# A score tile of 128 keys made by four matmuls of 32 keys, in the column tiling of the weighted sums

## The chip, the cores and the metric

One NeuronCore of a Trainium2 chip. The metric is the device time of one execution in microseconds (us). A core has a matrix engine (TensorE, PE in the profile; its weight loads are PEld), VectorE (DVE), ScalarE (ACT), GpSimd (POOL) and SyncE (SP, which only starts transfers). TensorE writes into eight PSUM banks of 128 partitions x 512 f32.

## The reference

Eight batches. `x` is (8, 1024, 512), the context (8, 2048, 512), 16 heads of 32.

```python
xn = layer_norm(layernorm(x), g1, b1);  cn = layer_norm(context, g2, b2)
q, k, v = xn @ Wq.T, cn @ Wk.T, cn @ Wv.T            # 16 heads of 32
scores = einsum('bqhs,bkhs->bhqk', q, k) / sqrt(32)  # masked keys: -inf
attn = softmax(scores);  out = einsum('bhqk,bkhs->bqhs', attn, v)
x = x + out @ Wo.T + bo
x = x + fp6_quantised(layernorm(x)) @ fp6_quantised(weight).T + bias
```

## The kernel before, in words

Each engine has its program written out by hand; semaphores (`wait_ge`, `then_inc`) are all that orders them. A batch has three stages: projections of queries, keys and values (`front`), attention, and output tiles with the quantised layer.

Attention goes in 8 **units** a batch: a group of four heads (`g`) times half of the queries (`q`, 512). A unit takes the 2048 keys in 16 **tiles** of 128, one `step` each. For one tile and four heads j:

- **scores** (`score(j)`, L947): one f16 matmul of 98 rows (a head's 32 dimensions in three split parts, and two rows for the mask and the maximum) by 128 keys, streaming 512 queries, into one bank.
- **exponentials** (L743, ScalarE), one for each score bank, into `PR[u]`, a ring of four f32 tiles.
- **weighted sums** (`outputs()`, L957): four f32 matmuls, one a head, each with 128 rows by 32 columns, head j writing partitions 32j to 32j+31 of the bank `OB`. The four are column tiles of the array. An f32 matmul stands as two records in the profile, so that a step has eight.
- **maxima** (`max_pair`, L923): two pairs of f16 matmuls of 33 rows by 128 columns, which compute part of the scores of a later unit, from which VectorE takes row maxima (L583). All units but the last need them for the next: in a batch 104 of the 128 steps have them, the last half of unit 6 and all of unit 7 don't.
- **row sums** (L983): four matmuls like the weighted sums, with ones for weights. GpSimd adds exponentials of two tiles in pairs (`pair`, L399) and merges the pairs with accumulating transfers (`merge`, L410, `merge_late`, L416), so that row sums are needed in only four steps of a unit. In the last step of a unit there are two `clear` matmuls (L989) beside them.

A step issues scores 0 and 1 of the next tile, weighted sums of this tile, scores 2 and 3 of the next, maxima, row sums. Score j waits until its bank's last exponential is made: for tiles under 8 there are two score banks, so that score 1 waits for exponential 3 of the tile before; for the others three. The weighted sums wait for all four exponentials of their tile. The exponentials of an even tile wait until GpSimd has added the pair that last used their buffers. A maxima pair waits for the reduction before the last (two pairs of banks). GpSimd issues the second late merge of a unit when the first has landed, and only then takes the next unit's pairs.

Of the kernel before, what the change touches and what calls it, by code (L numbers as in the profile page):

```python
# [8 lines left out]
P = 128  # L9


def ds(start, n):
    return slice(start, start + n)


HALF = 512
# [32 lines left out]
def build(nc, x, ctx_in, mask, wqT, wkT, wvT, woT, bo, affine_in, w, wb, out):  # L49
    B, T, D = x.shape  # L50
    C = ctx_in.shape[1]
    H, HD = 16, D // 16
# [53 lines left out]
    with ExitStack() as es:  # L106
# [3 lines left out]
        KA = sb("keys_stacked", [P, H * C], F16)  # L110
        QA = sb("queries_stacked", [P, NU * J * HALF], F16)
# [53 lines left out]
        def score_bank(tile, j):  # L165
            if tile < 8:
                return bank(4 + j % 2), 2
            slot = 4 * (tile - 8) + j + ((tile, j) >= (10, 2))
            return bank((7, 4, 5)[slot % 3]), 2 if tile == 10 and j >= 2 else 3
# [37 lines left out]
        s_st = sem("scores_made")  # L207
# [622 lines left out]
        def _(e):  # L830
# [13 lines left out]
            for b in range(0, B):  # L844
# [72 lines left out]
                STR = 3 * HD + 2  # L917

                def max_pair(parity, g, q, r, h):
                    a, t, c = piece(r, h)  # L920
                    for i in range(2):
                        rows = ds(2 * HD * i, HD + 1)
                        mm = e.matmul(MXB[parity][:, i, :],  # L923
                                      QA[rows, ds(((2 * g + q) * J + 2 * a + i) * HALF + t * P, P)],
                                      KA[rows, ds((g * J + 2 * a + i) * C + c * HALF, HALF)], start=True, stop=True)
                    mm.then_inc(s_mxf, 1)
# [5 lines left out]
                def step(m, ex, ka, qa, v, u, tile, row=None, after=None, sums=(), end=False, between=None, scores=True,  # L932
                         weigh=True, fresh=None, closing=False, turning=True):
                    if row:
                        count, *piece_of = row
                    if after:
                        e.wait_ge(*after)

                    def score(j):
                        if scores:  # L940
                            dst, back = score_bank(tile, j)
                            e.wait_ge(s_ex, ex + (u + 1) * J + j + 3 - back)
                            if tile == 8 and j == 0:
                                e.wait_ge(s_on, m + 1)
                            if tile == 11 and j == 0 and turning:
                                e.wait_ge(s_mc, m + 2)
                            e.matmul(dst, KA[0:STR, ds(ka + (j * C + (u + 1) * P), P)],  # L947
                                     QA[0:STR, ds(qa[j], HALF)], start=True, stop=True).then_inc(s_st, 1)

                    def max_part(h):  # L950
                        e.wait_ge(s_mxd, count + (h + 1))
                        max_pair(h, *piece_of, h)

                    def outputs():
                        e.wait_ge(s_ex, ex + (u * J + J + 2))
                        for j in range(J):
                            mm = e.matmul(OB[HD * j:HD * j + HD, :], V[:, ds(v + u * D + HD * j, HD)],  # L957
                                          PR[u][:, j * HALF:j * HALF + HALF], start=False, stop=end,
                                          skip_group_check=True)
                        return mm  # L960

                    score(0)
                    score(1)
                    if weigh:
                        mm = outputs()
                        if end:
                            mm.then_inc(s_po, 1)
                    if between:
                        between()
                    score(2)  # L970
                    score(3)
                    if not weigh:
                        return
                    if row:
                        max_part(0)
                        max_part(1)
                    if fresh:
                        clear(LB, *fresh)
                    for i, (src, ready) in enumerate(sums):
                        if ready:  # L980
                            e.wait_ge(*ready)
                        for j in range(J):
                            mm = e.matmul(LB[HD * j:HD * j + HD, :], ones[:, :], src[:, ds(j * HALF, HALF)],  # L983
                                          start=False, stop=closing and i == len(sums) - 1, skip_group_check=True)
                    mm.then_inc(s_pv, 1)

                def clear(bank, left, count):
                    e.wait_ge(left, count)
                    e.matmul(bank[:, 0:2], zeros[:, :], zeros[:, 0:2], start=True, stop=False,  # L989
                             skip_group_check=True)  # L990
# [120 lines left out]
```

## Time and profile before

| | |
|---|---|
| median of 3 runs | 4893.51 us (4892.85 to 4898.69) |
| the profiled execution | 4894.66 us, its span 4892.9 us |
| TensorE busy | 4593.8 us, 94% |
| VectorE, GpSimd, ScalarE busy | 69%, 61%, 58% |
| score matmuls (L947) | 4096 |
| mean granted TensorE clock | 0.986 of 2.4 GHz |

The span is from the first to the last instruction. A record's duration is longer than the time it keeps the engine, because matmuls are pipelined: the start of one to the start of the next is what a matmul costs in a row of its kind.

### The profile page before, as it was taken

What the parts mean: (1) busy time and instruction counts of PE and PEld (TensorE: products, weight loads), DVE (VectorE), ACT (ScalarE), POOL (GpSimd) and SP (SyncE); (2) the same over time, 40 slices, a digit from 0 to 9 for tenths busy, and PEclk for the clock granted to TensorE, in tenths of its full rate; (3) what the DMA queues carried; (4) which work ended last, traced back from release to release, by engine and by line L of the source; (5) the groups of instructions that cost most, each with busy time, mean ns of one, the idle gap of its engine ahead of it and who ended that gap; (6) DMA issues with size and microseconds to landing.
All of it is one profiled execution on the core that took longest, in us unless ns stands there. A gap on an engine that the chain in (4) does not pass through costs nothing.

```text
span 4892.9 us, 65384 instructions
## 1 busy us (share of the span) xinstructions
PE 4593.8 (94%) x24720; PEld 1348.4 (28%) x24720; DVE 3379.8 (69%) x3943; ACT 2838.0 (58%) x5128; POOL 2971.8 (61%) x1818
## 2 busy tenths in 40 slices
PE   4999899998999989999899998999989999899998
PEld 2322242222422224222242222422224222342222
DVE  4788457884588855888357884588855887458873
ACT  3477634775347753477544774457744577446773
POOL 2278743777438773387634876347863578625875
PEclk9999999999999999999999999999999999999999
DMA  5255632555325553355533555335543355443552
GB/s 182 64 118 104 147 113 60 118 111 152 99 65 105 119 147 102 70 104 118 141 102 71 111 110 140 104 72 117 108 134 109 73 116 112 127 113 80 106 119 75
DMA packets 189918, 530.81 MB, mean 108 GB/s; under 512 B 28625, under 2 KB 102673, under 8 KB 148386
## 3 DMA queue, kind: packets, MB, share of 16 engines
q0 software_dynamic: 43776, 318.79, 32.3%
q1 hardware_dynamic: 145826, 207.83, 13.8%
q8 instruction: 195, 3.19, 0.3%
q14 instruction: 121, 0.99, 0.1%
HBM read 110.98 MB, written 21.01 MB: 27 GB/s over the span
## 4 chain that ended last, share of the span: by engine, by line
PE 75%; ACT 10%; DVE 6%; SPq 3%; DMA 3%; issue 2%; POOL 1%; ACTq 0%; DVEq 0%; POOLq 0%
PE banks L957 21%; PE banks L947 19%; PE banks L864 12%; PE banks L923 9%; PE banks L858 7%; ACT region L743 7%; PE banks L983 5%; DVE max_parts L583 3%; SPq L293 3%; PE banks L833 2%; DMA region<-in_x 1%; DVE region L574 1%; ACT values L814 1%; ACT region L718 0%; POOL wkT_wvT_wqT L399 0%
## 5 line engine op out<-in xcount | busy, mean ns | idle before, releaser
L583 DVE TENSOR_REDUCE max_parts<-banks 128x2 f32<-128x1024 f32 x2048 | 2400.1, 1218 | 469.2 <-PE banks L923 468.2
L743 ACT ACTIVATE region<-banks 128x512 f32<-128x512 f32 x4096 | 2211.0, 596 | 695.9 <-PE banks L947 656.9
L399 POOL TENSOR_TENSOR wkT_wvT_wqT<-region 128x1024 f32<-128x1024 f32 x608 | 1474.7, 2549 | 556.5 <-ACT region L743 554.3
L947 PE MATMUL banks<-queries_stacked,keys_stacked 98*128 98x512 f16 x4096 | 1298.4, 387 | 82.2 <-ACT region L743 50.7
L957 PE MATMUL banks<-region,values 128*32 128x512 f32 x8192 | 1100.6, 609 | 18.5 <-ACT region L743 7.7
L947 PEld LDWEIGHTS banks<-queries_stacked,keys_stacked 98*128 98x128 f16 x4096 | 289.0, 97 | 1438.7 <-ACT region L743 1356.4
L923 PE MATMUL banks<-keys_stacked,queries_stacked 33*128 33x512 f16 x4096 | 658.7, 384 | 7.0 <-DVE max_parts L583 3.5
L864 PE MATMUL banks<-region,wkT_wvT_wqT 128*128 128x512 f16 x2304 | 574.6, 388 | 48.1 <-POOL region L380 23.0
L601 DVE RECIPROCAL row_sums_inverse<-row_sums_inverse 128x128 f32<-128x128 f32 x256 | 232.0, 930 | 437.9 <-ACT row_sums_inverse L760 437.9
L399 POOL TENSOR_TENSOR sums<-region 128x1024 f32<-128x1024 f32 x160 | 395.7, 2631 | 25.7 <-ACT region L743 25.5
L574 DVE SCALAR_TENSOR_TENSOR region<-banks,region 128x512 f16<-128x512 f32 x192 | 132.2, 689 | 346.7 <-ACT region L726 345.7
L864 PE MATMUL banks<-wkT_wvT_wqT,region 128*128 128x512 f16 x1536 | 369.1, 380 | 0.0
L399 POOL TENSOR_TENSOR wdT<-region 128x1024 f32<-128x1024 f32 x128 | 314.4, 2595 | 1.5 <-ACT region L743 0.4
L923 PEld LDWEIGHTS banks<-keys_stacked,queries_stacked 33*128 33x128 f16 x4096 | 159.6, 93 | 559.9 <-issue 298.0
L726 ACT ACTIVATE region<-banks 128x512 f16<-128x512 f32 x192 | 113.7, 597 | 343.0 <-PE banks L864 286.2
L380 POOL TENSOR_TENSOR region<-row_sums_inverse,region 128x512 f16<-128x512 f32 x80 | 92.5, 1156 | 339.9 <-ACT region L718 339.9
L864 PEld LDWEIGHTS banks<-region,wkT_wvT_wqT 128*128 128x128 f16 x2304 | 214.6, 100 | 302.8 <-issue 65.0
L858 PE MATMUL banks<-wdT,values 128*128 128x512 f32 x512 | 249.8, 633 | 48.2 <-ACT values L814 48.2
L730 ACT ACTIVATE values<-banks 128x512 f32<-128x512 f32 x128 | 76.4, 597 | 334.0 <-PE banks L864 334.0
L858 PE MATMUL banks<-woT,queries_stacked 128*128 128x512 f32 x512 | 245.2, 627 | 26.3 <-DVE region L667 26.3
L416 POOL DMA_DIRECT2D wdT<-wkT_wvT_wqT x96 | 99.9, 1040 | 275.9 <-ACT region L743 155.3
L957 PEld LDWEIGHTS banks<-region,values 128*32 128x32 f32 x8192 | 161.6, 108 | 380.7 <-ACT region L743 219.3
(83 smaller groups left out, 2905.3 us busy)
## 6 DMA issues: line engine op xcount, KB each, us to landing
wdT<-wkT_wvT_wqT POOLq DMA_DIRECT2D x96, 1024.0 KB, 11.4
wkT_wvT_wqT<-wkT_wvT_wqT POOLq DMA_DIRECT2D x80, 1024.0 KB, 7.0
sums<-wkT_wvT_wqT POOLq DMA_DIRECT2D x72, 1024.0 KB, 7.0
keys_stacked<-region SPq DMA_DIRECT2D x768, 64.0 KB, 2.0
wkT_wvT_wqT<-sums POOLq DMA_DIRECT2D x40, 1024.0 KB, 7.0
region<-in_x SPq DMA_DIRECT2D x24, 1024.0 KB, 10.0
wkT_wvT_wqT<-weights_split SPq DMA_DIRECT2D x8, 3072.0 KB, 19.3
queries_stacked<-region SPq DMA_DIRECT2D x384, 64.0 KB, 2.0
```

Source lines behind the costliest of these rows:

```text
L293: e.dma_start(dst, KS[HD * j:HD * j + HD, part, gs, :]).then_inc(s_kd[h], 16)
L399: e.tensor_tensor(SUMS[dst][:, half], PR[i][:, half], PR[i + 1][:, half], ALU.add).then_inc(s_pr, 1)
L574: e.scalar_tensor_tensor(KS[:, 1, i, :], PJB[j % 2], 1.0 / W_SCALE, KS[:, 0, i, :], ALU.mult, ALU.subtract).then_inc(s_k2, 1)
L583: e.tensor_reduce(mpart[:, buf, :, a, t, c], MXB[parity], AX.X, ALU.max).then_inc(s_mxd, 1)
L601: inv = e.reciprocal(part, part)
L743: e.activation(PR[u % 4][:, j * HALF:j * HALF + HALF], score_bank(kt, j)[0], ACT.Exp, scale=SCALE).then_inc(s_ex, 1)
L858: mm = e.matmul(bank, lhs(cc), rhs(cc), start=(cc == 0), stop=(cc == CC - 1))
L864: mm = e.matmul(bank, lhs(p, cc), rhs(r, cc), start=(cc == 0 and i == 0), stop=(cc == CC - 1 and i == 2))
L923: mm = e.matmul(MXB[parity][:, i, :], QA[rows, ds(((2 * g + q) * J + 2 * a + i) * HALF + t * P, P)], KA[rows, ds((g * J + 2 * a + i) * C + ...
L947: e.matmul(dst, KA[0:STR, ds(ka + (j * C + (u + 1) * P), P)], QA[0:STR, ds(qa[j], HALF)], start=True, stop=True).then_inc(s_st, 1)
L957: mm = e.matmul(OB[HD * j:HD * j + HD, :], V[:, ds(v + u * D + HD * j, HD)], PR[u][:, j * HALF:j * HALF + HALF], start=False, stop=end, sk ...
L983: mm = e.matmul(LB[HD * j:HD * j + HD, :], ones[:, :], src[:, ds(j * HALF, HALF)], start=False, stop=closing and i == len(sums) - 1, skip_ ...
```

## The change

Each `score(j)` is issued as four matmuls of 32 keys. Matmul t takes the 32 key columns from 32t on and writes partitions 32t to 32t+31 of the same bank; rows, queries and result are what they were. The semaphore is raised by the last of the four. The waits stand ahead of the first. No other engine's program changes.

```diff
-                            e.matmul(dst, KA[0:STR, ds(ka + (j * C + (u + 1) * P), P)],
-                                     QA[0:STR, ds(qa[j], HALF)], start=True, stop=True).then_inc(s_st, 1)
+
+                            for t in range(P // HD):
+                                mm = e.matmul(dst[HD * t:HD * t + HD, :],
+                                              KA[0:STR, ds(ka + (j * C + (u + 1) * P + HD * t), HD)],
+                                              QA[0:STR, ds(qa[j], HALF)], start=True, stop=True)
+                            mm.then_inc(s_st, 1)
```

Here is how the matmuls stand on TensorE, at a unit's last step and the first steps of the next (columns of the output and queries streamed at the end; an f32 matmul is one row here). Before:

```order
L957 MATMUL banks<-region,values 32x512 x4
L947 MATMUL banks<-queries_stacked,keys_stacked 128x512 x2
L923 MATMUL banks<-keys_stacked,queries_stacked 128x512 x4
L989 MATMUL banks<-zeros 128x2
L983 MATMUL banks<-region,ones 32x512 x4
L989 MATMUL banks<-zeros 128x2
L947 MATMUL banks<-queries_stacked,keys_stacked 128x512 x2
L957 MATMUL banks<-region,values 32x512 x4
```

The same place with the change (L949 are the scores, L961 the weighted sums, L987 the row sums, L993 the clears):

```order
L961 MATMUL banks<-region,values 32x512 x4
L949 MATMUL banks<-queries_stacked,keys_stacked 32x512 x8
L923 MATMUL banks<-keys_stacked,queries_stacked 128x512 x4
L993 MATMUL banks<-zeros 128x2
L987 MATMUL banks<-region,ones 32x512 x4
L993 MATMUL banks<-zeros 128x2
L949 MATMUL banks<-queries_stacked,keys_stacked 32x512 x8
L961 MATMUL banks<-region,values 32x512 x4
```

Nothing stands elsewhere: two matmuls of 128 columns are eight of 32, between the same neighbours.

## Rows read from the trace of the kernel before

**Rows 1.** The page: engines' busy time, then groups (count, busy us, mean ns).

```profile
PE 4593.8 (94%) x24720; PEld 1348.4 (28%) x24720; DVE 3379.8 (69%) x3943; ACT 2838.0 (58%) x5128; POOL 2971.8 (61%) x1818
...
L947 PE MATMUL banks<-queries_stacked,keys_stacked 98*128 98x512 f16 x4096 | 1298.4, 387 | 82.2 <-ACT region L743 50.7
L957 PE MATMUL banks<-region,values 128*32 128x512 f32 x8192 | 1100.6, 609 | 18.5 <-ACT region L743 7.7
...
L858 PE MATMUL banks<-wdT,values 128*128 128x512 f32 x512 | 249.8, 633 | 48.2 <-ACT values L814 48.2
```

**Rows 2.** Timeline of TensorE, one step with maxima: start us, us spanned, count.

```profile
989.60 1.06 PE L957 MATMUL banks<-region,values 128*32 128x512 f32 x8
990.60 0.60 PE L947 MATMUL banks<-queries_stacked,keys_stacked 98*128 98x512 f16 x2
991.13 0.61 PE L923 MATMUL banks<-keys_stacked,queries_stacked 33*128 33x512 f16 x4
991.68 0.61 PE L947 MATMUL banks<-queries_stacked,keys_stacked 98*128 98x512 f16 x2
992.22 1.07 PE L957 MATMUL banks<-region,values 128*32 128x512 f32 x8
...
993.75 0.61 PE L923 MATMUL banks<-keys_stacked,queries_stacked 33*128 33x512 f16 x4
```

**Rows 3.** Timeline of TensorE, the closing row sums of a batch.

```profile
589.73 1.92 PE L983 MATMUL banks<-region,ones 128*32 128x512 f32 x16
...
594.05 1.04 PE L983 MATMUL banks<-sums,ones 128*32 128x512 f32 x8
```

**Rows 4.** Timeline of TensorE in the projections, f16 before f32 transposes.

```profile
2479.89 1.03 PE L864 MATMUL banks<-region,wkT_wvT_wqT 128*128 128x512 f16 x4
2480.75 0.60 PE L833 MATMUL banks<-ident,values 128*128 128x128 f32 x4
```

**Rows 5.** Timeline of all engines, steps without maxima: loads of the weighted sums.

```profile
1171.33 0.16 PEld L957 LDWEIGHTS banks<-region,values 128*32 128x32 f32 x8 [0.39 <-ACT region L743]
...
1173.89 0.16 PEld L957 LDWEIGHTS banks<-region,values 128*32 128x32 f32 x8 [0.39 <-ACT region L743]
...
1176.51 0.16 PEld L957 LDWEIGHTS banks<-region,values 128*32 128x32 f32 x8 [0.39 <-ACT region L743]
```

**Rows 6.** Timeline, a unit's last step, one with row sums, a two-bank one.

```profile
1002.97 1.07 PE L957 MATMUL banks<-region,values 128*32 128x512 f32 x8
...
1006.78 1.06 PE L957 MATMUL banks<-region,values 128*32 128x512 f32 x8
...
1010.38 1.06 PE L957 MATMUL banks<-region,values 128*32 128x512 f32 x8
...
1012.95 0.10 PEld L947 LDWEIGHTS banks<-queries_stacked,keys_stacked 98*128 98x128 f16 x1 [0.39 <-ACT region L743]
1013.27 0.16 PEld L957 LDWEIGHTS banks<-region,values 128*32 128x32 f32 x8 [0.23 <-issue]
```

**Rows 7.** Timeline, VectorE's reductions after the maxima of rows 2.

```profile
991.56 2.36 DVE L583 TENSOR_REDUCE max_parts<-banks 128x2 f32<-128x1024 f32 x2 [0.26 <-PE banks L923]
```

**Rows 8.** Busy time in one unit: window, us, busy (count) of PE, PEld, DVE, ACT, POOL, clock.

```profile
955.58:1002.97 47.39, 47.05 (x294) 10.29 (x293) 41.07 (x38) 35.88 (x68) 38.27 (x20) 1.00 0.55 112
```

**Rows 9.** Timeline of GpSimd, the late merges of two units, and its waits.

```profile
996.40 0.85 POOL L416 DMA_DIRECT2D wdT<-wkT_wvT_wqT  x1 [0.16 <-issue]
...
1010.04 0.87 POOL L416 DMA_DIRECT2D wdT<-wkT_wvT_wqT  x1 [8.09 <-DMA wdT<-wkT_wvT_wqT]
...
1038.14 4.67 POOL L399 TENSOR_TENSOR wkT_wvT_wqT<-region 128x1024 f32<-128x1024 f32 x2 [0.27 <-ACT region L743]
...
1043.35 1.19 POOL L416 DMA_DIRECT2D wdT<-wkT_wvT_wqT  x1
...
1090.73 1.14 POOL L416 DMA_DIRECT2D wdT<-wkT_wvT_wqT  x1
...
1102.65 0.87 POOL L416 DMA_DIRECT2D wdT<-sums  x1 [6.08 <-ACT region L743]
```

## The prediction

> **What bounds the kernel now.** I read the page first [rows 1]: TensorE is busy 94% of the span, and the score matmuls (L947) and weighted sums (L957) are its largest groups. That share doesn't say whether TensorE sets the pace, since ScalarE, VectorE and GpSimd hang on it in loops. So I read the timeline of a step of the attention stage, engine by engine, and looked for what closes each loop.
>
> A step with maxima, tiles 8 to 15 of a unit [rows 2]: weighted sums start at 989.60, scores 2 and 3 at 990.60, maxima at 991.13, the next scores 0 and 1 at 991.68, the next weighted sums at 992.22. The step is 2.62 us, its legs 1.00, 0.53, 0.55 and 0.54. The reader should see that none of them is what its matmuls alone cost. Two scores span 0.60 and one 0.38 (mean 387 ns) [rows 1, 2], so scores follow each other every 0.22; yet the next group starts 0.53 to 0.54 after the first score, not 0.44. The weighted sums take 1.00 before scores, but the same shape followed by itself takes less: at a batch's end row sums of the same shape follow each other in groups of 8 records, and the first five groups, from 589.73 to 594.05 [rows 3], take 4.32, 0.864 each. So 0.10 to 0.13 goes after each group whose successor has another shape: the array runs empty. Whole-array scores (98x128), maxima (33x128) and 32-column sums (128x32) are three shapes, and a step changes shape four times.
>
> Data type is not the reason: four whole-array f16 matmuls start at 2479.89, and the f32 transposes behind them at 2480.75, 0.86 = 4 x 0.215 later [rows 4], nothing lost.
>
> Three other loops lie just under 2.62, and decide how much can be gained:
> - **ScalarE.** The weighted sums need all four exponentials of the tile scored before. Without maxima between [rows 5]: the loads of the weighted sums, held by ScalarE, start at 1171.33, 1173.89 and 1176.51, steps of 2.56 and 2.62 in turn, 1.56 and 1.62 of them after scores 2 and 3 (1.00 goes before).
> - **ScalarE, two banks** (tiles under 8): score 1 waits for the last exponential. It starts at 1012.95 [rows 6], 1.57 after scores 2 and 3 (1010.38 + 1.00 = 1011.38); the sums follow 0.32 later at 1013.27. Step 2.89.
> - **VectorE.** The maxima at 991.13 [rows 2] feed two reductions that run from 991.56 for 2.36, to 993.92 [rows 7]. The next step's second maxima pair needs both: it starts 0.22 after 993.75 [rows 2], at 993.97. So first pair to second pair of the next step is 2.84, and from there to the first pair of the step after 2.62 - 0.22 = 2.40: two steps in 5.24, 2.62 a step. It is exactly tight.
>
> **The change, by its parts.** The order, the waits and all other engines' work stay. 4096 score matmuls become 16384, each with a weight load.
>
> (1) *Removed:* the shape change between scores and weighted sums, both ways, and between row sums and scores. Weighted sums to scores 1.00 becomes 0.87; scores to weighted sums 0.54 becomes 0.44. The changes at the maxima stay.
>
> (2) *Added:* four streams for one. The trace has no f16 matmul in column tiles. Its f32 ones run side by side: eight records span 1.06, where one takes 0.609 [rows 1, 2], two passes of 0.43 and 0.02 at most for the four starts. The bounds for a score are its 0.22 of now and the 0.43 of an f32 pass, which is a rival. I take the 0.22, since an f32 pass is no slower in column tiles (0.43) than in the whole array, and 0.02 more until the last tile has written, which ScalarE and the maxima wait for.
> The loads of the nearest shape ride under the stream before them: groups of 0.864 leave them no room of their own [rows 3]. Lost cover costs some 0.01 to 0.10, only behind the maxima. The Trainium skill (TensorEngine Tiling, Restrictions and Gotchas) speaks against the change here: column tiling rules out the fast weight load. No run here shows what that costs at f16.
>
> (3) *Sums by class of step.*
> - Tiles 8 to 15, eight steps of a unit. TensorE: 0.87 + 0.55 + 0.55 + 0.44 = 2.41. ScalarE: (1.62 + 1.56)/2 + 0.02 + 0.87 = 2.48. VectorE: (2.84 + 2.41 - 0.22)/2 = 2.515. Largest: 2.52, saved 0.10, x8 = 0.80. VectorE is late next.
> - Two banks, four steps: 1.57 + 0.02 + 0.22 + 0.87 = 2.68, saved 0.20, x4 = 0.80. ScalarE stays the bound.
> - With row sums, three steps: from 1006.78 to 1010.38, 3.60 [rows 6], all TensorE. Saved 0.13 + 0.13 + 0.10 - 0.02 = 0.34, x3 = 1.02.
> - The last step, 1002.97 to 1006.78 = 3.81 [rows 6], has the clears between sums and scores: saved 0.21.
> A unit of 47.39 [rows 8] would lose 2.83, to 44.56.
>
> (4) *Who was covered by that time.* GpSimd, busy 38.3 of the 47.4 [rows 8], also waits for a transfer in mid-unit. It issues the first late merge at 996.40, the second, which needs the first landed, at 1010.04, then starts on the next unit's pairs; the next first merge is at 1043.35 [rows 9], 46.95 later. In between it waited for ScalarE by 0.27 as shown (some 0.8 with the overlap of its records). So this loop alone is about 46.2, over 44.56. But the 13.64 from first to second late merge is long here; two units on, it is 1090.73 to 1102.65, 11.92 [rows 9], which makes 44.5. The mean of the two is 45.3. Buffers let GpSimd fall two or three us behind before exponentials wait for it, and each batch begins with it level. I charge 0.3 a unit: 2.5 saved.
>
> (5) *A batch.* Unit 0 has no row sums from before: 6 x 0.20 + 8 x 0.10 + 0.21 + 0.20 = 2.4. Units 1 to 5: 12.5. Unit 6, half without maxima (2.59 to 2.49 there): 2.4. Unit 7, without any: row-sum steps 3.60 - 0.54 = 3.06 fall to the 2.68 of ScalarE, 3 x 0.38 = 1.1; the others 3 x 0.20 + 9 x 0.10 = 1.5; less 0.3, 2.3. Sum 19.6, times 8 = 157. Projections and output tiles (the other 230 us of a batch) are not touched.
>
> The profiled execution took 4894.7, its span 4892.9; the median of the three runs is 4893.5, the same within 0.03%. 4893.5 - 157 = **4736**.
>
> **The rivals.**
> - *GpSimd and its merges take most of it.* If the transfers are as long as the 13.64 throughout and the slack is used up, a unit is 46.2: 1.2 saved, x7.5 x8 = 72, 4820. For: the first of the two units [rows 9]. Against: the second, and the slack. Chance 0.14.
> - *f16 column tiles stream at an f32 pass's rate, 0.43* (slower). A step with maxima becomes 0.87 + 0.43 + 0.53 + 0.22 + 0.32 + 0.43 + 0.43 = 3.23, +0.61, x8; the two-bank ones +0.35, x4; the row-sum ones +0.5, x4: +8.3 a unit, no loss without maxima; 6.5 units x 8 = +430, 5325. It turns a loss when a score takes over 0.30. Against: f32 runs at the same rate in column tiles (records of 609 ns) as in the whole array (L858, 633 ns [rows 1]), so tiling slows no stream that is shown. Chance 0.07.
> - *TensorE cannot be fed* (slower). A unit has 294 matmuls and 293 loads [rows 8], 81 ns each; it will have 486 and 485, in 44.6 us 46 ns each. The densest long stretch is 40 matmuls and their 40 loads in 4.32 us, 54 ns each [rows 3], and it was bound by its streams, so it shows no limit. If 54 were one: 971 x 0.054 = 52.4, +5.0 a unit, x 6.5 x 8: 5155. It decides from 47.39/971 = 49 ns. Chance 0.07. The Trainium skill (TensorE: Matmul & The Clock Gate, Back-to-back issue gap) gives 81 ns for a load and matmul with 128 columns, sustained: an estimate of 39 us for 486 pairs, which would not bind. No run here shows it.
> - *The array still empties*, because 98 rows or the f16 loads count as another shape: nothing saved, 0.02 added in places, 4895 to 4930. Against: 33x128 and 98x128 differ by rows in use (under a half against over it), 98 and 128 are on the same side. Chance 0.04.
>
> **How the numbers follow.** Forecast 0.68, from 4690 (VectorE's and GpSimd's loops looser than read, TensorE's 2.41 reached) to 4790. With the first rival 0.82 lies in 4690 to 4830; the range is that. Faster by over 0.2% (10 us, about what a measurement of this kernel can tell): 0.82. Within it: 0.03, half of the last rival and a little. Slower: 0.15.
>
> **What would show it.** Score records 32 columns wide, four starting within some 30 ns, and the next weighted sums 0.44 behind the first; weighted sums to scores 0.87; steps of 2.52 and 2.68; the row-sum steps at 3.27; more waits of the second maxima pair for VectorE, and of exponentials for GpSimd. A score of 0.30 or more, or sums to scores still at 1.00, would prove me wrong, as would matmuls that trickle in without a wait.

## The result

The changed kernel takes 4775.2 us (median of 4 runs, 4772.1 to 4777.8) against 4894.4 us (4 runs): a ratio of 0.9755, 95% interval 0.9738 to 0.9772. That is 119 us less, where 157 was forecast. The range held it; the sum was 39 us off.

The page of the profile after (span 4770.2 us): busy time, the chain that ended last, then groups. L949 is the scores, L961 the weighted sums.

```profile
PE 4450.3 (93%) x37008; PEld 1515.2 (32%) x37008; DVE 3533.2 (74%) x3943; ACT 2834.9 (59%) x5128; POOL 2975.5 (62%) x1818
...
PE 54%; POOL 15%; DMA 9%; ACT 7%; DVE 6%; issue 6%; SPq 3%; ACTq 0%; POOLq 0%; DVEq 0%
...
L949 PE MATMUL banks<-queries_stacked,keys_stacked 98*32 98x512 f16 x16384 | 1366.2, 385 | 94.3 <-ACT region L743 71.6
L961 PE MATMUL banks<-region,values 128*32 128x512 f32 x8192 | 1079.0, 601 | 20.0 <-ACT region L743 7.7
```

Beside [rows 1], four times the score records keep TensorE about as long (1366.2 us against 1298.4): the four run side by side. GpSimd and transfers now have 15% and 9% of the chain that ended last; before they had 1% and 3%.

Timeline of TensorE, the step that answers to [rows 2]:

```profile
965.83 1.07 PE L961 MATMUL banks<-region,values 128*32 128x512 f32 x8
966.71 0.62 PE L949 MATMUL banks<-queries_stacked,keys_stacked 98*32 98x512 f16 x8
967.26 0.69 PE L923 MATMUL banks<-keys_stacked,queries_stacked 33*128 33x512 f16 x4
967.88 0.62 PE L949 MATMUL banks<-queries_stacked,keys_stacked 98*32 98x512 f16 x8
968.33 1.03 PE L961 MATMUL banks<-region,values 128*32 128x512 f32 x8
969.19 0.60 PE L949 MATMUL banks<-queries_stacked,keys_stacked 98*32 98x512 f16 x8
```

Weighted sums to scores is 0.86 to 0.88 (1.00 before), scores to weighted sums 0.45 (0.54), scores to maxima 0.55 (0.53). Maxima to scores has grown from 0.55 to 0.62, and the four maxima span 0.69, not 0.61: the second pair waits for VectorE. The step is 2.50, where [rows 2] had 2.62.

Busy time by unit, batch 1, from unit to unit as in [rows 8] (window, us, then PE, PEld, DVE, ACT, POOL):

```profile
888.74:933.75 45.01, 44.92 (x489) 13.03 (x485) 40.97 (x38) 35.82 (x68) 37.59 (x20) 1.00 0.56 113
933.75:978.55 44.80, 44.76 (x489) 13.02 (x485) 40.97 (x38) 35.82 (x68) 36.88 (x21) 1.00 0.56 113
978.55:1024.99 46.44, 45.05 (x489) 12.99 (x484) 41.06 (x38) 35.76 (x68) 38.21 (x21) 1.00 0.57 114
1024.99:1071.18 46.19, 45.09 (x488) 12.94 (x484) 41.06 (x38) 35.87 (x68) 38.33 (x21) 1.00 0.57 115
1071.18:1116.39 45.21, 42.25 (x460) 12.34 (x456) 38.74 (x30) 35.13 (x68) 38.25 (x21) 1.00 0.58 117
1116.39:1161.99 45.60, 38.02 (x414) 10.41 (x407) 20.91 (x5) 34.87 (x66) 37.79 (x19) 0.96 0.64 131
```

The first units take 44.8 to 45.0, about what TensorE, ScalarE and VectorE allow among themselves (44.8, as a run below shows); then they grow, with the same work on each engine. The last unit has no maxima and should be the shortest; it takes 45.60, more than the 44.50 that it took before (this row is of the kernel before):

```profile
1144.95:1189.45 44.50, 38.86 (x225) 8.13 (x224) 4.81 (x5) 34.55 (x66) 36.10 (x18) 1.00 0.62 125
```

What holds them is seen in the timeline of GpSimd and ScalarE after:

```profile
975.11 0.85 POOL L416 DMA_DIRECT2D wdT<-wkT_wvT_wqT  x1
...
988.23 0.87 POOL L416 DMA_DIRECT2D wdT<-wkT_wvT_wqT  x1 [7.55 <-ACT region L743]
988.84 4.96 POOL L399 TENSOR_TENSOR sums<-region 128x1024 f32<-128x1024 f32 x2
...
993.84 2.25 ACT L743 ACTIVATE region<-banks 128x512 f32<-128x512 f32 x4 [1.12 <-POOL sums L399]
994.49 0.10 PEld L949 LDWEIGHTS banks<-queries_stacked,keys_stacked 98*32 98x32 f16 x4 [1.27 <-ACT region L743]
```

The first late merge is issued at 975.11, the second, which waits for it to land, at 988.23, and the next unit's first pair stands behind it until 988.84. Exponentials of an even tile need that pair's buffers, start at 993.84 after ScalarE has stood idle for 1.12, and the loads of the next scores follow them at 994.49, TensorE's load queue idle for 1.27. Over the whole run the waits of exponentials for GpSimd are 48.7, 36.5 and 8.7 us (94 together, by the buffer written) where the kernel before had 4.2 and 0.5. The 988.23 row names ScalarE as what released it, but the first late merge landed at 987.69, 0.54 ahead of the second, and the program waits for that landing.

### The profile page after: what moved, and what is told of

Same layout as the page of the kernel before. It is cut to its first block, busy times and chain, and to the rows that moved or that the text cites. A ratio compares the mean times of both kernels' runs of the same rounds, so it can differ in the third digit from the quotient of the medians.

```text
span 4770.2 us, 89960 instructions
## 1 busy us (share of the span) xinstructions
PE 4450.3 (93%) x37008; PEld 1515.2 (32%) x37008; DVE 3533.2 (74%) x3943; ACT 2834.9 (59%) x5128; POOL 2975.5 (62%) x1818
## 4 chain that ended last, share of the span: by engine, by line
PE 54%; POOL 15%; DMA 9%; ACT 7%; DVE 6%; issue 6%; SPq 3%; ACTq 0%; POOLq 0%; DVEq 0%
PE banks L949 11%; PE banks L961 11%; PE banks L864 11%; POOL wkT_wvT_wqT L399 9%; PE banks L858 8%; PE banks L923 7%; DMA wdT<-wkT_wvT_wqT 7%; ACT region L743 4%; DVE max_parts L583 4%; PE banks L987 3%; SPq L293 3%; POOL sums L399 2%; PE banks L833 2%; DMA region<-in_x 1%; POOL wdT L399 1%
## 5 line engine op out<-in xcount | busy, mean ns | idle before, releaser
L399 POOL TENSOR_TENSOR wkT_wvT_wqT<-region 128x1024 f32<-128x1024 f32 x608 | 1522.6, 2741 | 456.9 <-ACT region L743 455.9
L949 PE MATMUL banks<-queries_stacked,keys_stacked 98*32 98x512 f16 x16384 | 1366.2, 385 | 94.3 <-ACT region L743 71.6
L961 PE MATMUL banks<-region,values 128*32 128x512 f32 x8192 | 1079.0, 601 | 20.0 <-ACT region L743 7.7
L949 PEld LDWEIGHTS banks<-queries_stacked,keys_stacked 98*32 98x32 f16 x16384 | 416.4, 95 | 1323.7 <-ACT region L743 1034.1
L923 PE MATMUL banks<-keys_stacked,queries_stacked 33*128 33x512 f16 x4096 | 696.9, 384 | 6.7 <-DVE max_parts L583 3.5
L399 POOL TENSOR_TENSOR sums<-region 128x1024 f32<-128x1024 f32 x160 | 405.8, 2749 | 0.5
L923 PEld LDWEIGHTS banks<-keys_stacked,queries_stacked 33*128 33x128 f16 x4096 | 178.2, 93 | 557.2 <-issue 334.0
L399 POOL TENSOR_TENSOR wdT<-region 128x1024 f32<-128x1024 f32 x128 | 332.8, 2876 | 0.2 <-ACT region L743 0.2
L961 PEld LDWEIGHTS banks<-region,values 128*32 128x32 f32 x8192 | 211.8, 109 | 249.4 <-ACT region L743 185.7
L416 POOL DMA_DIRECT2D wdT<-wkT_wvT_wqT x96 | 110.9, 1155 | 286.1 <-ACT region L743 191.0
```

The lines of the kernel that those rows point to most:

```text
L399: e.tensor_tensor(SUMS[dst][:, half], PR[i][:, half], PR[i + 1][:, half], ALU.add).then_inc(s_pr, 1)
L923: mm = e.matmul(MXB[parity][:, i, :], QA[rows, ds(((2 * g + q) * J + 2 * a + i) * HALF + t * P, P)], KA[rows, ds((g * J + 2 * a + i) * C + ...
L949: mm = e.matmul(dst[HD * t:HD * t + HD, :], KA[0:STR, ds(ka + (j * C + (u + 1) * P + HD * t), HD)], QA[0:STR, ds(qa[j], HALF)], start=True ...
```

## The experiments

Each was compared with the kernel before on the same chip. The theory has two parts: (A) the array empties between matmuls of different shape, so what was gained hangs on both neighbours having the same one; (B) most of what did not come was lost to GpSimd's chain of pairs and late merges. What the records show of (A) is the time from one group's start to the next one's; that the array stands empty in the difference is my reading of it, since the ends of matmul records are modelled. The runs were spread over more than one chip, so that a difference between two of them is good to a few us: by their ratios to the kernel before, the 53, 20 and 14 us below are 51, 18 and 17.

**Scores 0 and 1 alone.**

```diff
-                            for t in range(P // HD):
+                            w = HD if j < 2 else P
+                            for t in range(P // w):
...
```

> Only scores 0 and 1 of a tile (the ones just ahead of the weighted sums) are made of four matmuls of 32 keys; scores 2 and 3 stay whole. Theory (the array empties at each change of shape, 0.10 us behind scores, 0.13 behind 32-column sums): the changes from scores 0, 1 to the weighted sums and from row sums to scores 0, 1 go, that from the weighted sums to scores 2, 3 stays at 1.00. Two-bank steps 2.89 - 0.09 = 2.80, row-sum steps 3.60 - 0.22 = 3.38, the eight others 2.59 (ScalarE's loop is untouched): 1.35 us less in a unit, about 78 us in all, 4815 us. Rival (smaller matmuls overlap better whatever stands beside them): half of the full gain of 119, 4835, and the weighted sums to scores leg gets shorter too.

Measured 4809.9 us, ratio 0.9832 (0.9817 to 0.9846), 83 less. Timeline of TensorE:

```profile
984.64 0.61 PE L950 MATMUL banks<-queries_stacked,keys_stacked 98*32 98x512 f16 x8
985.12 1.06 PE L962 MATMUL banks<-region,values 128*32 128x512 f32 x8
986.12 0.61 PE L950 MATMUL banks<-queries_stacked,keys_stacked 98*128 98x512 f16 x2
```

The leg into the sums is 0.48 (0.43 to 0.49 in that unit wherever nothing waits). The one out of them, whose shapes still differ, is 1.00 here and 0.96 to 1.00 in the unit. Small pieces on its other side did not bring it near 0.87.

**Scores 2 and 3 alone.** The same edit with `w = P if j < 2 else HD`.

> Only scores 2 and 3 of a tile (the ones just behind the weighted sums) are made of four matmuls of 32 keys; scores 0 and 1 stay whole. Theory (change of shape): weighted sums to scores 2, 3 becomes 0.86, scores 0, 1 to weighted sums stays at 0.54, row sums to scores 0, 1 stays at 1.00. Two-bank and row-sum steps lose 0.11 each, the eight others 0.06 (VectorE's loop (2.84 + 2.51 - 0.22)/2 = 2.56): 1.4 us a unit, about 80 us in all, 4813 us. Rival (smaller matmuls overlap better): 4835.

Measured 4812.4 us, ratio 0.9836 (0.9817 to 0.9854), 81 less. Timeline of TensorE:

```profile
984.87 0.61 PE L950 MATMUL banks<-queries_stacked,keys_stacked 98*128 98x512 f16 x2
985.41 1.06 PE L962 MATMUL banks<-region,values 128*32 128x512 f32 x8
986.29 0.62 PE L950 MATMUL banks<-queries_stacked,keys_stacked 98*32 98x512 f16 x8
```

Mirrored: 0.54 in, 0.88 out. The two halves together are 164, more than the 119 of the whole change. Half a change leaves GpSimd more time: units with maxima are 46.0 and 46.1 us long, and the waits of exponentials for GpSimd are 18 and 19 us over the run, where the whole change has 94.

**Two matmuls of 64 keys.** `w = 2 * HD` for all scores.

> Each score tile is made of two matmuls of 64 keys in column tiles of 64. Theory (change of shape): 128x64 is another shape than the sums' 128x32, all changes stay, nothing is gained: 4890 to 4920 us, weighted sums to scores still 1.00, scores to weighted sums 0.54. Rival (what helps is that a score is cut into pieces that load and stream side by side): at least half of the gain of 119, 4835 or less.

Measured 4917.1 us, ratio 1.0052 (1.0035 to 1.0068): 0.5% slower, small but clear of the noise. Timeline of TensorE:

```profile
984.22 0.62 PE L950 MATMUL banks<-queries_stacked,keys_stacked 98*64 98x512 f16 x4
984.77 1.06 PE L962 MATMUL banks<-region,values 128*32 128x512 f32 x8
985.76 0.62 PE L950 MATMUL banks<-queries_stacked,keys_stacked 98*64 98x512 f16 x4
986.32 0.61 PE L923 MATMUL banks<-keys_stacked,queries_stacked 33*128 33x512 f16 x4
```

The legs are 0.55 and 0.99, those of whole scores. Column tiles of 64 beside column tiles of 32 cost what the whole array beside them costs; pieces by themselves gain nothing; a unit is 47.80 where it was 47.39 [rows 8]. This was the sharpest test of (A).

**The second late merge put off,** in the changed kernel.

```diff
...
                         pair(0, first)
+                        if g + q > 0:
+                            put_off()
...
                         if not end:
-                            merge_late(1, 6, two)
+                            put_off = lambda f=merge_late, src=two: f(1, 6, src)
```

> The changed kernel, and GpSimd issues the second late merge of a unit after the first pair of the next unit, not before it, so that it does not stand waiting for the first late merge to land with that pair behind it. Theory (the part of the forecast that did not come, 39 us, was mostly lost to GpSimd's chain of pairs and late merges): units with maxima at 44.8 us, no waits of exponentials for GpSimd (85 us in all before), the long step of 4 to 5.2 us in the last unit gone: 40 us less, 4735 us. Rival (the rest was lost on TensorE, VectorE and ScalarE; GpSimd's waits lie in their shadow): within 8 us of 4775.

Measured 4722.0 us, ratio 0.965 (0.9635 to 0.9664): 171 less than before, 53 less than the change alone. Units of batch 1, the same ones as above:

```profile
924.57:969.36 44.79, 44.75 (x489) 13.04 (x485) 40.98 (x38) 35.82 (x68) 38.30 (x20) 1.00 0.59 119
969.36:1014.15 44.79, 44.74 (x488) 13.03 (x484) 40.98 (x38) 35.81 (x68) 38.32 (x20) 1.00 0.59 119
...
1103.65:1145.36 41.71, 36.23 (x415) 10.32 (x407) 4.87 (x5) 34.67 (x66) 36.17 (x18) 1.00 0.68 140
```

Every unit with maxima throughout is back at 44.8, the last unit is at 41.71. Of the waits of exponentials for GpSimd 2.6 us are left. Now GpSimd's first pair waits for ScalarE, not for a transfer (timeline of GpSimd):

```profile
963.47 0.85 POOL L416 DMA_DIRECT2D wdT<-wkT_wvT_wqT  x1 [0.16 <-issue]
964.06 4.98 POOL L399 TENSOR_TENSOR wkT_wvT_wqT<-region 128x1024 f32<-128x1024 f32 x2
974.26 4.68 POOL L399 TENSOR_TENSOR sums<-region 128x1024 f32<-128x1024 f32 x2 [5.22 <-ACT region L745]
978.89 0.87 POOL L416 DMA_DIRECT2D wdT<-wkT_wvT_wqT  x1
```

(B) is shown, and it is larger than I had said: 53 us where 40 were expected. This version beats both kernels.

**The same edit in the kernel before.**

> The kernel before, whole score matmuls, with GpSimd's second late merge put off behind the first pair of the next unit, as in the run e4_late_merge_put_off. Theory (GpSimd's chain had slack in the kernel before and became a bound only when the change shortened the units): no change, within 6 us of 4893. Rival (putting the merge off helps by itself, whatever the scores do): some 50 us less, 4840, as it was between the changed kernel and that run.

Measured 4894.3 us against 4896.4, ratio 0.9998 (0.9989 to 1.0008): nothing. GpSimd's wait was covered in the kernel before; the change took the cover away.

**Maxima cut to 32 columns too,** in the changed kernel.

```diff
...
-                        mm = e.matmul(MXB[parity][:, i, :],
+                        for k in range(P // HD):
+                            mm = e.matmul(MXB[parity][HD * k:HD * k + HD, i, :],
...
```

> The changed kernel, and each maxima matmul (33 rows x 128 columns) is issued as four of 32 columns too. A unit then has about 1355 TensorE records (matmuls and loads) where the changed kernel has 971. It keeps its own shape (33 rows, not 98), so no change of shape goes. Theory (feeding TensorE is no bound at 46 ns a record, and the gain needs the same rows and columns on both sides): 4775 to 4800, legs from scores to maxima still 0.54. Rival (TensorE is close to what its instruction supply gives): units of 62 us at 46 ns a record, over 5500 us. Rival (any column tile of 32 is the same shape, whatever its rows): the changes at the maxima go too, legs 0.44, and some 10 to 20 us less.

Measured 4795.1 us, ratio 0.9792 (0.9778 to 0.9807), 20 more than the change alone. Timeline of TensorE, then a window of it (PE and PEld are the first two):

```profile
986.90 0.61 PE L950 MATMUL banks<-queries_stacked,keys_stacked 98*32 98x512 f16 x8
987.44 0.76 PE L924 MATMUL banks<-keys_stacked,queries_stacked 33*32 33x512 f16 x16
```

```profile
940.00:990.00 50.00, 50.00 (x756) 14.99 (x748) 45.56 (x42) 40.12 (x76) 41.34 (x22) 1.00 0.60 120
```

Two things follow. Over 50 us, 1504 records pass, 33 ns each, so the 46 that the change needs was no bound, and the rival of a starved TensorE is out. And the leg from scores to maxima stays 0.54: 33 rows by 32 columns is not the shape of 98 rows by 32. Rows count as well as columns, though not every difference of rows does: 98 beside 128 cost nothing. The 20 us lie in the units themselves: those in which nothing waits for GpSimd take 45.14 where the changed kernel's take 44.80, and 0.34 in each of 52 units with maxima (6.5 in each of 8 batches) is 18. Pieces that match no neighbour cost here too, as those of 64 keys did.

**Faster reductions,** in the kernel with the merge put off.

```diff
-... MXB[parity], AX.X, ALU.max)
+... MXB[parity][:, :, 0:HALF // 2], AX.X, ALU.max)
```

> The kernel with the late merge put off, and VectorE takes row maxima over only 256 of each 512 scores of a maxima bank; the other half is left out, so that its time is read as that of a kernel with faster reductions. Theory (VectorE's loop of 2.515 us holds the eight steps of tiles 8 to 15, ScalarE's loop of 2.48 lies next under it): those steps go from 2.51 to 2.48 in the mean, row-sum and two-bank steps lose a little where the second maxima pair waited: 10 to 25 us less than 4722, about 4705. Rival (VectorE is not in the way at all): 4722 within 5 us. Rival (VectorE is the main bound): steps of TensorE's own 2.41, over 45 us less.

Measured 4708.0 us, ratio 0.9616 (0.96 to 0.9632): 14 less than 4722. The view of waits of that run still has this line, where the one with whole reductions had 204.0 us in 683 waits:

```profile
PEld banks L925 <- DVE max_parts L585: 10.2, 24, 0.4
```

and a unit of it is

```profile
924.57:969.18 44.61, 44.49 (x490) 12.28 (x488) 24.30 (x37) 35.81 (x68) 38.28 (x20) 1.00 0.59 120
```

The 204 us of waits were worth some 14. A unit is 0.18 shorter, which is 9 us over 52 units; the rest is not in these units, and I can't say where it is. VectorE's loop was the longest of three, but ScalarE's lay close under it, as the sums of 2.515 and 2.48 said.

## Why the prediction was right, and where it was off

- **Change of shape, 0.10 behind scores and 0.13 behind sums: right.** Legs of 0.45 and 0.86 to 0.88; each half of the change shows its own leg alone. The price is measured; that it is the array running empty stays a reading.
- **f16 column tiles at full rate: right.** A score costs 0.22 still, the eight records of two scores span 0.62 where two whole ones span 0.60 (0.02 for the four starts, as charged). Loss of the fast weight load, which the Trainium skill's page on tiling (TensorEngine Tiling, Restrictions and Gotchas) speaks of, does not show in these legs.
- **Steps: nearly right.** In the unit from 933.75 the two-bank steps take 2.67, 2.67, 2.67 and 2.73 (forecast 2.68), the last 3.58 (3.60), the eight of tiles 8 to 15 between 2.46 and 2.72, 2.56 in the mean (2.52), the three with row sums 3.39, 3.36 and 3.25 (3.27). The unit was put at 44.56, and 44.8 came. The steps with row sums are the largest miss; here is one of 3.39, at the start of the next unit:

```profile
982.13 1.03 PE L961 MATMUL banks<-region,values 128*32 128x512 f32 x8
982.99 0.75 PE L949 MATMUL banks<-queries_stacked,keys_stacked 98*32 98x512 f16 x8
983.34 0.10 PEld L949 LDWEIGHTS banks<-queries_stacked,keys_stacked 98*32 98x32 f16 x4 [0.39 <-ACT region L743]
...
984.21 1.06 PE L987 MATMUL banks<-region,ones 128*32 128x512 f32 x8
985.09 0.62 PE L949 MATMUL banks<-queries_stacked,keys_stacked 98*32 98x512 f16 x8
985.52 1.04 PE L961 MATMUL banks<-region,values 128*32 128x512 f32 x8
```

  Scores 2 and 3 span 0.75, not 0.62, since the loads of score 3 (983.34) now wait for ScalarE's exponential of the bank. The prediction called these steps "all TensorE" and took 0.34 off each; shortened by that much they run into ScalarE. The 0.24 a unit that were missed are about 12 us in all.
- **GpSimd: the mechanism was right, its size wrong.** This is the term that was mis-sized: "I charge 0.3 a unit", which stands in seven units of a batch, some 17 us in all. The run with the merge put off puts it at 53. Where it went is seen when the units of the two runs are set side by side, from clear matmul to clear matmul, over all eight batches. Units 1 to 5 take 45.21 in the mean against 44.82: 0.4 a unit, 15 us in all, so that the charge was about right there. Unit 6, half without maxima, takes 45.10 against 44.20, 7 us in all. The last unit takes 44.58 against 41.31, 26 us in all, and is longer than in the kernel before (43.96). It has the shortest steps and so the least cover, and was charged 0.3 like the others.

  Two more things go into it. The time from first to second late merge, put at a mean of 12.8 from two units, is 12.7 over all 56 of the kernel before, but 13.2 over all 56 of the changed one, since the landing takes longer there; in the batch shown it goes up to 13.7, and its units 4 and 5 take 46.44 and 46.19, about the 46.2 of the first rival. And I took two or three us of slack as I read them before the change; whether they had shrunk with the steps was not measured.
- **Luck.** Without any charge the sum would have been about 174, and 171 came with the merge put off. That is closer than the terms were: the steps of units 1 to 5 gave 2.6 a unit, not 2.83, 10 us less in all, and the first unit of a batch gave 3.75 in the mean over the batches where 2.4 was forecast, 11 us more in all. Why the first unit gave more was not looked into.
- **The rivals.** The first, GpSimd taking most of it (4820), came in part: 53 of 171. The slower two are out: scores at full rate, and 33 ns a record when more were there. The 81 ns for a load and matmul that the prediction took from the Trainium skill (TensorE: Matmul & The Clock Gate, Back-to-back issue gap) are for matmuls that stream 128 columns, and these stream 512, so that the estimate of 39 us did not apply; the run with more records gives 66 ns for such a pair. The fourth rival is out as well: no leg is longer for f16 beside f32, nor for 98 rows beside 128 (0.86 and 0.45).

## What to carry to other kernels

Count the changes of shape (rows and columns of the stationary tile) in TensorE's order, not only the matmuls: here each cost 0.10 to 0.13 us between groups of 0.4 to 0.9 us, and cutting a whole-array matmul into column tiles removed one for some 0.02, since the four stream together. It pays only when columns and rows match the neighbour's, where 98 and 128 rows passed as the same, and 33 beside 98 did not; 64 columns beside 32 gained nothing and cost 0.5%. When all loops of a pipeline lie within a few per cent of the longest, price the next one with its own waits for transfers, above all in the stage with the shortest steps, since a wait that was covered becomes the bound: half of what GpSimd took here it took in one unit of eight.

## What was not expected of the hardware

Weight loads and matmuls passed at 33 ns a record over 50 us (1504 records), with TensorE's granted clock at 1.00 throughout. And pieces are not free where they change nothing: two matmuls of 64 keys for one of 128 made a unit 0.41 us longer.

GpSimd's lateness also cost clock. In the last unit of batch 1 after the change, TensorE's busy time and its granted clock (the third figure from the end) went like this:

```profile
1128.00:1131.00 3.00, 1.85 (x20) 0.33 (x12) 0.00 (x0) 1.09 (x2) 3.00 (x2) 1.00 1.07 216
1131.00:1134.00 3.00, 1.55 (x20) 0.47 (x20) 0.00 (x0) 2.17 (x4) 3.00 (x3) 0.94 0.46 93
1134.00:1137.00 3.00, 2.73 (x24) 0.64 (x20) 0.00 (x0) 1.72 (x4) 2.70 (x3) 0.50 0.00 0
1137.00:1140.00 3.00, 3.00 (x40) 0.80 (x32) 0.00 (x0) 2.10 (x5) 3.00 (x3) 0.99 0.75 150
```

TensorE stood for some 2.6 of 6 us while exponentials waited for GpSimd; then the clock was 0.50 of 2.4 GHz, 1.2, for about 3 us, although TensorE was busy again. That unit's mean is 0.96; with the merge put off, and in the kernel before, it is 1.00 in all eight batches. Three of the eight last units after the change, from clear to clear:

```profile
1117.85:1162.99 45.14, 37.56 (x407) 10.24 (x403) 21.91 (x5) 33.44 (x64) 36.90 (x19) 0.96 0.64 133
1704.11:1747.42 43.31, 36.22 (x406) 10.08 (x403) 22.00 (x5) 33.33 (x64) 36.44 (x19) 1.00 0.64 131
4051.85:4099.80 47.95, 40.36 (x406) 10.86 (x403) 4.84 (x5) 33.46 (x64) 36.94 (x19) 0.89 0.60 125
```

In four batches the clock fell in the last unit (0.96 three times, 0.89 once), and it took 44.6 to 48.0 us; in the four where it stayed at 1.00, 42.8 to 44.3. The same matmuls kept TensorE busy for 37.56 us in the first of these rows and for 36.22 in the second. The Trainium skill (TensorE: Matmul & The Clock Gate, Part 1) tells of this fall and its two levels, and the trace agrees with its 1.2 GHz. Some 1.3 of the 3.9 us by which that unit is longer than with the merge put off (45.60 against 41.71) can be this, an estimate from the two busy times; the forecast had not counted it.

VectorE has 153 us more of busy time after the change (3533.2 against 3379.8), though its program is the same. Nearly all of it is one product of a unit's results with the inverse row sums; here it is in batch 1, after and before:

```profile
1144.46 18.65 DVE L608 TENSOR_TENSOR queries_stacked<-queries_stacked,row_sums_inverse 128x512 f32<-128x512 f32 x1
1171.12 1.42 DVE L608 TENSOR_TENSOR queries_stacked<-queries_stacked,row_sums_inverse 128x512 f32<-128x512 f32 x1
```

GpSimd added pairs almost without a gap while the long one ran. The 24 such products take 216.7 us together after the change, 61.2 before, and 30.9 with the merge put off, where GpSimd has its waits for ScalarE between pairs. No run takes the cause apart, and the view shows nothing that waited for the long ones.
